# Loading x in two halves, turning its first tiles one by one, keeping router logits in PSUM, and a new order on four engines

## What is computed

```python
mod = silu(c) @ wmod                      # six vectors of 128: sa, ca, ga, sb, cb, gb
ga = (2 * (ga >= 0) - 1) * max(abs(ga), 0.25)   # and the same for gb
h = layernorm(x) * (1 + ca) + sa
q = (h @ Wq + bq) / sqrt(128); k = h @ Wk + bk; v = h @ Wv + bv
x = x + ga * (softmax(causal(q @ k.T)) @ v @ Wo + bo)
h = layernorm(x) * (1 + cb) + sb
mask = top 4 of 16 blocks of softmax(h @ w_router + b_router)   # per token
y = relu(h @ w1.T + b1) * mask_per_channel @ w2.T + b2          # 16 blocks of 32 channels
x = x + gb * y
```

## Time and profile before

| What | Value |
|---|---|
| Time, median of 3 runs (lowest to highest) | 119.22 us (119.22 to 119.25) |
| The profiled execution's own time | 119.25 us |
| Its span in the profile | 117.4 us |
| Busy PE, PEld | 111.6 us (95%), 87.7 us (75%) |
| Busy DVE, ACT, POOL | 89.6 us (76%), 76.0 us (65%), 88.8 us (76%) |
| Chain that ended last, by engine | PE 60%, DVE 21%, POOL 6%, issue 4%, ACT 3%, DMA 3% |
| DMA | 3.42 MB, nearly all of the reading in the first 10.5 us |

### The profile page before, as it was taken

The page is one execution under the profiler, slowest core; times in us unless marked ns, Lnnn a source line. Parts: engine busy times, 40 slices in busy tenths (PEclk is TensorE's granted clock), DMA queues, the critical chain, the costliest instruction groups (busy, mean ns, idle before and its releaser), DMA issues.

```text
span 117.4 us, 1999 instructions
## 1 busy us (share of the span) xinstructions
PE 111.6 (95%) x587; PEld 87.7 (75%) x587; DVE 89.6 (76%) x312; ACT 76.0 (65%) x162; POOL 88.8 (76%) x122
## 2 busy tenths in 40 slices
PE   5999998999999999999999999999998999999980
PEld 2488777877888888878787878778777887855770
DVE  5579999998898989999895489715898836894431
ACT  2326887768945697975889997498632696436430
POOL 6587979679996999999969999959992897812000
PEclk9999999999999999999999999999999999999999
DMA  1994000000000000000000000000000000006033
GB/s 39 244 366 115 3 0 0 6 3 0 3 0 0 6 0 0 0 0 3 0 0 0 6 0 0 0 0 0 0 0 6 3 0 3 0 0 179 6 89 89
DMA packets 6274, 3.42 MB, mean 29 GB/s; under 512 B 1141, under 2 KB 5878, under 8 KB 6263
## 3 DMA queue, kind: packets, MB, share of 16 engines
q1 hardware_dynamic: 5830, 3.09, 9.1%
q10 hardware_dynamic: 432, 0.20, 0.6%
HBM read 2.24 MB, written 1.05 MB: 28 GB/s over the span
## 4 chain that ended last, share of the span: by engine, by line
PE 60%; DVE 21%; POOL 6%; issue 4%; ACT 3%; DMA 3%; DVEq 0%; ACTq 0%
PE bank L841 16%; PE bank L845 14%; PE bank L842 14%; PE bank L884 6%; PE bank L955 3%; DMA cols<-in_L_c_dram 3%; DVE chosen L755 2%; POOL p_lo L467 2%; DVE swung_sums L729 2%; DVE marked L747 2%; DVE hid_full L764 2%; DVE keys L738 1%; DVE st L629 1%; PE bank L1043 1%; PE bank L865 1%
## 5 line engine op out<-in xcount | busy, mean ns | idle before, releaser
L467 POOL TENSOR_TENSOR p_lo<-p_full,p_hi 128x512 fp32r<-128x512 f32 (+2 forms) x36 | 43.3, 1224 | 5.1 <-ACT p_full L570 5.1
L563 ACT ACTIVATE p_hi<-bank 128x512 fp32r<-128x512 f32 (+2 forms) x36 | 20.6, 572 | 6.9 <-PE bank L845 3.0
L570 ACT ACTIVATE p_full<-bank 128x512 f32<-128x512 f32 (+2 forms) x36 | 20.6, 572 | 2.5 <-POOL p_lo L467 2.4
L473 POOL TENSOR_TENSOR hid_lo<-hid_full,hid_hi 128x512 fp32r<-128x512 f32 x12 | 15.4, 1290 | 6.1 <-ACT hid_hi L597 6.0
L669 DVE TENSOR_REDUCE cmax<-bank 128x1 f32<-128x512 f32 x24 | 16.2, 685 | 1.1 <-PE bank L884 0.6
L841 PE MATMUL bank<-g_hi,zt_hi 128*128 128x512 f32 (+3 forms) x40 | 15.1, 379 | 0.4 <-DVE back L802 0.4
L884 PE MATMUL bank<-zt_hi,g_hi 128*128 128x512 f32 (+3 forms) x40 | 15.0, 391 | 0.1
L845 PE MATMUL bank<-g_lo,zt_hi 128*128 128x512 f32 (+3 forms) x40 | 14.6, 365 | 0.0
L842 PE MATMUL bank<-g_hi,zt_lo 128*128 128x512 f32 (+3 forms) x40 | 14.6, 364 | 0.0
L841 PE MATMUL bank<-p_hi,z_hi 128*128 128x512 f32 (+2 forms) x36 | 14.1, 392 | 0.0
L845 PE MATMUL bank<-p_lo,z_hi 128*128 128x512 f32 (+2 forms) x36 | 13.5, 376 | 0.0
(11 more groups left out here) (190 smaller groups left out, 259.0 us busy)
## 6 DMA issues: line engine op xcount, KB each, us to landing
x<-in_L_attn_y_all_dram SPq DMA_DIRECT2D x4, 256.0 KB, 3.8
out_dram<-res SPq DMA_DIRECT2D x3, 256.0 KB, 2.4
w<-in_L_ffn_w_dram SPq DMA_DIRECT2D x2, 256.0 KB, 4.7
wmod<-in_L_wmod_dram SPq DMA_DIRECT2D x1, 256.0 KB, 4.5
out_dram<-res SPq DMA_DIRECT2D x2, 128.0 KB, 1.8
wmod<-in_L_wmod_dram ACTq DMA_DIRECT2D x1, 128.0 KB, 3.7
wk<-in_L_attn_Wk_dram SPq DMA_DIRECT2D x1, 64.0 KB, 3.3
wq<-in_L_attn_Wq_dram ACTq DMA_DIRECT2D x1, 64.0 KB, 3.5
```

The costliest lines, as they stand in the source:

```text
L467: pool.tensor_tensor(p_lo[:, s, w:], p_full[:, n % 2, w:], p_hi[:, s, w:].bitcast(F32), ALU.subtract).then_inc(p_lo_pool, 1)
L473: pool.tensor_tensor(hid_lo[:, m, :], hid_full[:, n % 2, :], hid_hi[:, m, :].bitcast(F32), ALU.subtract).then_inc(hid_lo_pool, 1)
L563: nc.scalar.activation(p_hi[:, s, w:], src, ACT.Exp).then_inc(p_hi_s, 1)
L570: nc.scalar.activation(p_full[:, n % 2, w:], src, ACT.Exp).then_inc(p_full_s, 1)
```

## The change

x of group 0 is loaded by two DMAs of two tiles each, the first with a semaphore of its own. The statistics of tiles 0 and 1 wait for the first, those of tiles 2 and 3 for the second. VectorE's a0 raises a semaphore after each tile, and TensorE's n0 waits tile by tile. The router's logits are written into a free part of the PSUM bank that holds the sums, in place of the SBUF tensor `logit`, and read from there. All four plans are replaced; TensorE's has four filler words fewer (i12 to i15).

```diff
@@ -39,30 +39,28 @@
 UNDER = -87.33
 
 TENSOR_PLAN = """
-i0 i1 i2 z0 i3 i4 i5 i6 i7 z1 i8 i9 i10 i11 i12 i13 i14 i15 z2 z3 n0 z6 z8 z4 q0 n1 a0 a1 z9 a2 q1 a3 z7 a4 b0
-z5 a5 n2 a6 a7 s0 a8 a9 s1 q2 a10 s2 a11 w0 a12 s3 b1 w1 a13 n3 a14 s4 a15 w2 a16 s5 a17 a18 s6 a19 s7 a20 w3
-a21 s8 a22 s9 a23 w4 s10 w5 o0 w6 q3 s11 b2 w7 a24 w8 a25 s12 a26 w9 a27 s13 a28 s14 a29 w10 a30 w11 s15 s16
-a31 s17 a32 w12 a33 w13 s18 o1 s19 n4 w14 a34 a35 s20 w15 w16 a36 s21 a37 s22 a38 w17 a39 w18 s23 w19 b3 w20
-r0 w21 s24 w22 w23 s25 s26 h0 s27 m0 w24 s28 n5 s29 o2 s30 w25 s31 w26 r1 s32 w27 h1 w28 s33 s34 w29 m1 w30
-w31 s35 s36 n6 s37 h2 w32 h3 s38 s39 r2 w33 w34 w35 w36 w37 w38 w39 h4 h5 m2 d0 o3 d1 d2 d3 h6 h7 d4 d5 y0 h8
-h9 d6 n7 h10 h11 r3 d7 h12 d8 d9 m3 y1 h13 v12 v13 d10 d11 h14 v14 h15 v15 d12 d13 d14 y2 d15 d16 d17 d18 d19
-y3 y4
+i0 i1 i2 z0 i3 i4 i5 i6 i7 z1 n0 i8 i9 z2 i10 i11 z6 z3 z8 q0 z9 n1 a0 z4 a1 a2 q1 a3 z5 a4 z7 a5 b0 a6 n2 a7
+s0 a8 a9 s1 q2 a10 s2 a11 w0 a12 s3 b1 w1 a13 n3 a14 s4 a15 w2 a16 s5 a17 s6 a18 w3 a19 s7 s8 o0 w4 s9 w5 a20
+a21 s10 q3 a22 w6 a23 w7 a24 w8 b2 s11 a25 w9 w10 a26 s12 a27 s13 a28 w11 a29 s14 a30 s15 a31 s16 w12 o1 w13
+s17 s18 a32 a33 w14 s19 a34 a35 s20 w15 s21 a36 w16 a37 n4 a38 s22 s23 a39 w17 w18 w19 b3 w20 r0 w21 s24 w22
+s25 w23 s26 s27 w24 m0 o2 s28 n5 s29 w25 w26 h0 s30 s31 r1 s32 h1 s33 w27 w28 w29 s34 m1 h2 s35 w30 n6 w31 s36
+h3 h4 s37 r2 s38 w32 s39 w33 w34 w35 w36 h5 w37 w38 w39 d0 d1 o3 d2 m2 d3 h6 h7 d4 d5 y0 h8 h9 d6 n7 d7 h10 r3
+d8 d9 y1 h11 m3 h12 h13 v12 v13 d10 d11 h14 v14 h15 v15 d12 y2 d13 d14 d15 d16 d17 d18 d19 y3 y4
 """
 SCALAR_PLAN = """
-z0 z1 z3 n0 a1 q0 n1 z4 z6 z12 q1 a2 z9 z5 z8 n2 e0 q2 e1 a3 e2 e3 e4 n3 e5 e6 c0 e7 e8 q3 e9 e10 e11 e12 e13
-e14 c1 e15 a4 e16 e17 z7 e18 e19 e20 e21 n4 e22 a5 e23 e24 c2 e25 e26 m0 e27 e28 n5 e29 e30 h0 e31 e32 a6 h1
-e33 m1 e34 e35 n6 e36 e37 e38 h2 h3 e39 c3 h4 h5 y0 m2 h6 h7 a7 h8 n7 h9 h10 y1 h11 m3 h12 h13 y2 h14 h15 y3
-y4
+z0 z1 n0 z3 z6 a1 q0 n1 z8 z4 q1 z5 a2 z9 z12 n2 e0 e1 q2 a3 e2 e3 e4 n3 e5 c0 e6 e7 e8 e9 q3 e10 e11 e12 e13
+c1 e14 e15 e16 e17 e18 a4 e19 e20 e21 z7 n4 e22 e23 a5 e24 c2 e25 e26 m0 e27 e28 n5 e29 e30 h0 e31 a6 e32 e33
+h1 m1 e34 e35 n6 h2 e36 e37 e38 e39 h3 c3 h4 h5 m2 y0 h6 h7 a7 h8 n7 h9 y1 h10 m3 h11 h12 h13 y2 h14 h15 y3 y4
 """
 VECTOR_PLAN = """
-g0 z1 g1 a0 g2 z10 z3 z11 n0 g3 q0 s0 n1 s1 s2 s3 q1 s4 b0 s5 z5 s6 s7 n2 s8 s9 s10 s11 s12 b1 s13 s14 s15 s16
-s17 s18 s19 s20 s21 s22 i8 s23 n3 q2 x0 i9 i10 b2 s24 i11 s25 s26 s27 s28 g4 s29 s30 s31 q3 s32 s33 z6 x1 g5
-s34 s35 i20 s36 s37 i21 s38 s39 i22 n4 b3 i23 m0 c0 h0 x2 n5 g6 m1 c1 h1 i36 n6 h2 i37 i38 h3 m2 i39 c2 h4 h5
-x3 g7 h6 h7 h8 h9 n7 h10 m3 c3 h11 f0 f1 k12 k13 k14 k15 f2 f3 f4
+g0 z1 a0 g1 n0 g2 z3 z10 z11 g3 q0 s0 n1 s1 s2 s3 q1 s4 z5 s5 b0 s6 s7 n2 s8 s9 s10 s11 s12 b1 s13 s14 s15 s16
+s17 s18 s19 q2 n3 i8 x0 i9 s20 s21 i10 s22 s23 s24 b2 s25 i11 s26 s27 s28 s29 s30 s31 g4 q3 x1 z6 s32 s33 g5
+s34 i20 s35 s36 i21 s37 s38 i22 i23 s39 n4 b3 m0 c0 x2 n5 g6 h0 m1 c1 h1 h2 n6 i36 h3 m2 i37 h4 i38 i39 c2 h5
+x3 g7 h6 h7 h8 h9 n7 h10 m3 c3 f0 h11 f1 k12 k13 k14 k15 f2 f3 f4
 """
 GPSIMD_PLAN = """
-z7 z0 z1 z5 z4 p0 p1 p2 u0 z6 p3 u1 l0 l1 z8 l2 u2 l4 l5 u3 l6 l7 z11 l8 l9 l10 z10 l12 l13 p4 l14 l15 l16 l17
-l18 p5 l19 l20 l21 l22 z9 l24 l25 l26 l27 l28 l29 l30 p6 k0 l31 l32 l33 l34 l35 k1 l36 l37 l38 k2 k3 k4 k5 p7
+z0 z5 p0 z1 z7 p1 u0 z6 p2 z8 u1 p3 l0 l1 z4 l2 u2 l4 l5 l6 l7 l8 l9 l10 z11 u3 z10 l12 l13 l14 l15 l16 p4 l17
+l18 l19 p5 l20 l21 l22 z9 l24 l25 l26 l27 l28 l29 p6 l30 l31 k0 l32 l33 k1 l34 k2 l35 l36 l37 l38 k3 k4 k5 p7
 k6 k7 k8 k9 k10 k11
 """
 
@@ -214,7 +212,6 @@
 
 
         swung_sums = sb("swung_sums", [P, GT, 2, NBLK])
-        logit = sb("logit", [P, GT, NBLK])
         lmax = sb("lmax", [P, GT])
         keys = sb("keys", [P, GT, KEYS])
         top8 = sb("top8", [P, GT, 8])
@@ -226,6 +223,7 @@
             sem(n) for n in ("c_loaded", "wmod1_loaded", "wmod2_loaded", "wq_loaded", "wk_loaded", "wv_loaded", "wo_loaded"))
         bias_qk_in_s, bias_vo_in_s, w1_in_s, b1_in_s, w2_in_s, wr_in_s, b2_in_s = (
             sem(n) for n in ("bias_qk_loaded", "bias_vo_loaded", "w1_loaded", "b1_loaded", "w2_loaded", "router_loaded", "b2_loaded"))
+        x_first_s, first_applied = sem("x_first_loaded"), sem("first_applied")
         stored = [sem(f"stored{g}") for g in range(NG)]
 
         ident_made, copies_made, causal_made, future_made, unseen_made, warm_made, filler_made, base_made, ones_made, keys_made, spread_made = (
@@ -280,8 +278,10 @@
             return grp(first if n < NG else second, n % NG)
 
         def norm_applied(n):
+            if n == 0:
+                return first_applied, GT
             by_act = scalar_applies(n)
-            return xn_by_act if by_act else xn_by_dve, sum(scalar_applies(k) == by_act for k in range(n + 1))
+            return xn_by_act if by_act else xn_by_dve, sum(scalar_applies(k) == by_act for k in range(1, n + 1))
 
         def one_turn(g):
             return g in ONE_TURNS
@@ -343,7 +343,8 @@
             def load_x(g):
                 load(tokens(x, g), x_tiles[g], x_in_s[g])
 
-            load_x(0)
+            for i in range(2):
+                load(x[:, 2 * i:2 * i + 2, :], x_tiles[0][:, 2 * i:2 * i + 2, :], x_in_s[0] if i else x_first_s)
             load(wk[:], wk_in, wk_in_s)
             load_column(BQ, bq_in, bias_qk_in_s)
             load_column(BK, bk_in, bias_qk_in_s)
@@ -621,11 +622,13 @@
             def norm_stats(n):
                 k, g = n // NG, n % NG
                 s = slice(g * GT, (g + 1) * GT)
-                if k == 0:
+                if n > 0 and k == 0:
                     dve.wait_ge(x_in_s[g], 16)
-                else:
+                elif k == 1:
                     dve.wait_ge(turn_out, turn_of[f"o{g}"] + 2)
                 for i in range(GT):
+                    if n == 0 and i % 2 == 0:
+                        dve.wait_ge(x_in_s[0] if i else x_first_s, 16)
                     last = nc.vector.bn_stats(st[:, k, g * GT + i, :], x[:, g * GT + i, :])
                 step(last)
                 for i in range(GT):
@@ -645,7 +648,10 @@
                     t = g * GT + i
                     last = nc.vector.tensor_scalar(norm_rows(n)[:, i, 1:], x[:, t, 1:], mv[:, k, t, 0:1],
                                                    rstd[:, k, t:t + 1], ALU.subtract, ALU.mult)
-                last.then_inc(xn_by_dve, 1)
+                    if n == 0:
+                        last.then_inc(first_applied, 1)
+                if n > 0:
+                    last.then_inc(xn_by_dve, 1)
 
             def norm_low(n):
                 dve.wait_ge(nt_hi_s, n + 1)
@@ -732,10 +738,11 @@
                     sums = swung_sums[:]
                 if g == 0:
                     dve.wait_ge(keys_made, 1)
-                step(nc.vector.tensor_reduce(logit[:], sums.rearrange("p i s e -> p i e s"), AX.X, ALU.add))
-                step(nc.vector.tensor_reduce(lmax[:], logit[:], AX.X, ALU.max))
+                logit = sums_bank(g)[:, GW // 2:GW // 2 + GT * NBLK].rearrange("p (i e) -> p i e", i=GT)
+                step(nc.vector.tensor_reduce(logit, sums.rearrange("p i s e -> p i e s"), AX.X, ALU.add))
+                step(nc.vector.tensor_reduce(lmax[:], logit, AX.X, ALU.max))
                 most = lmax[:].rearrange("p (i o) -> p i o", o=1).broadcast_to([P, GT, NBLK])
-                nc.vector.scalar_tensor_tensor(out=keys[:, :, 0:NBLK], in0=most, scalar=UNDER, in1=logit[:], op0=ALU.add,
+                nc.vector.scalar_tensor_tensor(out=keys[:, :, 0:NBLK], in0=most, scalar=UNDER, in1=logit, op0=ALU.add,
                                                op1=ALU.max).then_inc(keys_s, 1)
 
             def choose(g):
@@ -850,18 +857,21 @@
                     pe.wait_ge(turn_out, n - 1)
 
             def turn_norm(n):
-                pe.wait_ge(*norm_applied(n))
-                if n == 0:
+                if n > 0:
+                    pe.wait_ge(*norm_applied(n))
+                else:
                     pe.wait_ge(ident_made, 1)
                     pe.wait_ge(ones_made, 1)
-                elif n < NG:
+                if 0 < n < NG:
                     pe.wait_ge(nt_lo_s, n)
                 elif n == NG:
                     pe.wait_ge(nt_lo_s, NG)
                     pe.wait_ge(ones_made, 2)
-                else:
+                elif n > NG:
                     pe.wait_ge(keep_s, n - NG)
                 for i in range(GT):
+                    if n == 0:
+                        pe.wait_ge(first_applied, i + 1)
                     last = nc.tensor.transpose(tile(norm_bank, i), norm_rows(n)[:, i, :], ident[:])
                 last.then_inc(xt_mm, 1)
 
```

## The result

The changed kernel takes 118.78 us, median of 12 runs (118.48 to 120.4), against 119.27 us for the kernel before in the same session. The ratio is 0.9952, with a 95% interval of 0.9934 to 0.9970. The forecast was 119.7 us and slower; the kernel became 0.5% faster. The profiled execution took 118.82 us with a span of 117.1 us.

The account below looks back on a forecast made before the run. A GpSimd, VectorE and ScalarE chain bounds up to TensorE's first score s0, then TensorE's fixed work plus waits. 119.25 + 1.45 - 1.09 + 0.15 = 119.76 us, 0.03 above the median, so 119.7 us predicted; range 118.4 to 120.7.

Parts of the forecast that it names:

- the named late waits: TensorE's waits for group 2's choice, group 3's choice and ScalarE's copy of the latter: 0.47, 0.40, 0.22 us, all to go.
- The start: Up to TensorE's first score s0: g1 behind a0 delays p1, a1 and q0; s0 +1.45 us, at 20.4, bounds +0.75 to +1.9.
- the block of lift1 by GpSimd: VectorE's z1 at the start: lift1 waits for p0's power operation until 6.98, so a0 starts at 7.45; 0.45 us.
- the rest of the reordering behind s0: Order changes after the first score that rows couldn't cost: taken as 0, between -0.5 and +0.5 us.
- The waits from q0 to s0: Steps in the way on ScalarE and TensorE may make q1 late ahead of s0: 0.25 us, between 0 and 0.7.
- The late weight: SyncE's later loads: one weight TensorE now wants earlier (w1, for z6) may come late, priced at 0.3 us.
- The gain meant for the path: At the start, a0 ahead of g1 lets n0's high half start after about 8.9 in place of 10.17, over 1 us.
- After s0: Behind the first score: named waits go, -1.09 us, at the least -0.2; new waits +0.15; other reordering 0.
- The new wait of 0.15 us at h13: On TensorE, h13 needs h11's bank, and f0 (0.7 us) stands ahead of h11 on VectorE: +0.15 us.
- (1): Rival: GpSimd bounds the middle since z4 falls into it and late low halves hold TensorE; 120.7 us, chance 0.16.
- (2): Rival: faster, new order removes TensorE's many small waits between 20 and 113 us, exceeding s0's loss; 118.4 us, chance 0.27.
- (3): Rival: lift1 isn't blocked, a0 starts at 7.0, s0 +1.0 us; end 119.15 us, no difference that can be told, chance 0.15.

Follow-up runs that it names:

- the square: Four kernels, logits in PSUM, start and rest each old or new: old/old 118.87 us, old/new 118.11, new/old 119.48, new/new (the changed kernel) 118.78.
- the run with g1 first: Changed kernel with one swap on VectorE, the statistics g1 again ahead of a0: 119.32 us, ratio 0.9996 to the kernel before.
- the whole load: Changed kernel with x of group 0 loaded by one DMA again, all else as changed: 119.01 us, ratio 0.9979 to the kernel before.
- the run with a0 first: Kernel with PSUM logits and new orders only behind router step r0, plus p0 ahead of z4 and a0 ahead of g1: 118.56 us, ratio 0.9936.
- all old orders: Changed kernel with all four orders of the kernel before; half loads, tile by tile transposes and PSUM logits remain: 118.99 us, ratio 0.9967.
- p0 first: Kernel with PSUM logits and new orders only behind router step r0, plus p0 ahead of z4 on GpSimd: 117.99 us, ratio 0.9889.
- the crossed runs: Two kernels with PSUM logits, plans exchanged at TensorE's s0: kernel before with new plans behind it, 118.11 us; changed kernel with old plans behind it, 119.48 us.
- old start and new rest: Kernel before with PSUM logits and the changed kernel's plans from TensorE's first score s0 on: 118.11 us, ratio 0.9898 to the kernel before.
- new from r0 on: Kernel before with PSUM logits and new orders only behind TensorE's router step r0: 117.70 us, ratio 0.9867 to the kernel before.
- the second splice: Kernel before with PSUM logits, new order from s0 to score s15, old order from there to r0, new behind: 122.30 us, ratio 1.0224.
- new start and old rest: Changed kernel up to TensorE's first score s0, then the plans of the kernel before, with PSUM logits: 119.48 us, ratio 1.0013.

## Why the prediction was wrong

**What bounds the kernel** was right: what s0 loses the end loses, as the square shows, and the named late waits were on the path.

**Which steps failed.** Two terms of the sum were wrong, both towards a slower kernel. The start was put at +1.45 us and measured +1.01 in the trace and 0.6 to 0.7 in the medians; within it the block of lift1 by GpSimd, 0.45 us, didn't take place. And the rest of the reordering behind s0 was put at nothing, where the trace shows some 0.4 us of gain, group 1's choice and the turn of norm 6 above all. In the traces either error alone would have left about no change (+1.45 - 1.36 = +0.09, +1.01 - 0.94 = +0.07), and both together give the gain. In the medians the start alone turns the sign (+0.6 - 0.94 = -0.3).

**The start** had the right sign and, but for the block, the right mechanism, and was mis-sized. Forecast for s0 was +1.45 us (bounds 0.75 to 1.9); the trace shows +1.01, and medians of whole runs 0.6 to 0.7. Step by step: a0 was put at 7.45 and came at 7.15, g1's end at 9.80 and came at 9.45, a1 at 12.0 and came at 11.53. The step that failed is the block of lift1 by GpSimd's power operation, 0.45 us. In the run with g1 first lift1 started at 5.90, took 0.36 us and ended well inside the power operation of 5.61 to 6.66: no block. With the whole load it is the same (lift1 from 6.47 for 0.36 us, the power operation from 6.25 to 7.30), and so with lift2 in the run with a0 first (from 10.85 for 0.34 us, inside the operation of 10.25 to 11.29). In the changed kernel itself the two don't overlap: lift1 started at 6.81, after the power operation's end at 6.68, and was late for another reason, TensorE's first preparation. The row on which I priced it, the keys operation, is a wait for an operation on 128x512; the power operation is on 128x4. The rule of the Trainium skill (SBUF — State Buffer, section Who interferes with whom), that a VectorE instruction with two SBUF inputs contends with a GpSimd instruction that reads SBUF, fits keys, which was held with two such inputs and took 0.22 us each time with one of them in PSUM. For lift1, which names one SBUF tensor twice, these traces don't agree with it. Whether the double name or the small operation is the reason wasn't tried. The two may not be wholly free of each other: where lift1 began 0.12 or 0.13 us ahead of the power operation, the latter took 1.14 and 1.13 us in place of 1.05 (all old orders, p0 first). The waits from q0 to s0, taken at 0.25 us, measured 1.01 - 0.79 = 0.22. Why whole runs lose less than the first score isn't shown; the last section has what the rows say.

That x of group 1 is covered held for the changed kernel, whose g1 doesn't wait for it. The late weight priced at 0.3 us came: in the changed kernel TensorE waits 0.37 us for w1 at 9.74, and in the old orders 0.30 us for wmod. That either moves s0 isn't shown, and the first hardly can, for q0 comes only at 11.51. The gain meant for the path, a0 1.1 us earlier, was worth nothing, as said.

**After s0** the forecast was -1.09 of named waits and +0.15 of new ones, -0.94 us together. Measured from s0 to y4: -1.36 by the trace (-0.35 - 1.01), and -1.1 by the medians (logits 0.4 and rest 0.7). The three named waits went, but they were worth 0.9 and not 1.09, since for two of them 0.23 us was taken as the distance without a wait where it is 0.32. The new wait of 0.15 us at h13 didn't come (104.43 stands 0.24 us behind 104.19). Left out was group 1's choice, and the turn of norm 6 behind it. In the kernel before:

```profile
73.61 1.46 DVE L755 TENSOR_SCALAR chosen<-marked 128x512 bf16<-128x512 f32 x1
...
74.66 0.39 PE L845 MATMUL bank<-p_lo,z_hi 128*128 128x512 f32 x1
75.13 0.40 PE L991 MATMUL bank<-ident_b,chosen 128*128 128x128 bf16 x4
...
78.19 0.60 PE L865 MATMUL bank<-ident,xn 128*128 128x128 f32 x4
78.83 0.45 PE L841 MATMUL bank<-g_hi,zt_hi 128*128 128x384 f32 x1
```

Here chosen takes 1.46 us, where it takes 0.43 in the changed kernel, and m1 waits 0.47 - 0.23 = 0.24 us for it. Behind the turn of norm 6 the next product comes after 0.64 us, in the changed kernel after 0.35. From r0 to m1 the changed kernel saves 0.44 us, and from m1 to n7 0.8 where 0.47 was counted. Both waits could have been costed from the kernel before as the three were; that the first would go could not, since it hangs on the 0.09 us by which chosen comes ahead of GpSimd. The other way there was a loss, 0.44 us from s0 to r0.

**The rivals.** (1) z4 in GpSimd's full stretch costs nothing against z8: the crossed runs stay in step. The loss from s0 to r0 was there, though, 0.44 us; part of it is one wait for a low half, the mechanism of this rival with another cause. TensorE's third pass comes at 59.07, 0.52 us behind the second (58.55), so 0.29 us late; p5, which the new order has one low half later, ends at 57.78 on GpSimd, just ahead of that half. In the list of waits of the changed kernel between 48 and 62 us it stands with the weight load (us in total, times, longest):

```profile
PEld bank L852 <- POOL p_lo L468: 0.6, 1, 0.6
```

The rest of that loss stays open. (2) was right in kind: the waits saved after s0 exceeded what s0 lost. It was given 118.4 us and a chance of 0.27. (3) was right that lift1 isn't blocked and that s0 moves by 1.0 us, and its time of 119.15 was nearer than the forecast; what it lacked is the gain of the reordering behind r0. With the distances of the trace in place of the terms the sum is 119.25 + 1.01 + 0.44 - 0.44 - 0.81 - 0.55 = 118.90. That it comes within 0.1 us of the profiled 118.82 is no test of the account, since the five distances add up to the shift of y4.

## What to carry to other kernels

When whole orders change, compare the start times of steps ahead of which both orders have done the same set of work; each stretch between them can be priced and swapped by itself, and the best of both may beat either. A splice has to keep every chain that runs over several engines in one order. Moving a step out of a hole to bring another forward pays only if nothing behind it waits for the step that was moved. Cost every wait of the bounding engine of the same kind (here all the choices and the turns of the norms), not only the largest ones, and take the distance without a wait from a product of the same form.

## What the hardware showed beyond that

The early clock of TensorE moves the start. Its filler products of 512 columns start 0.43 us apart at first (2.07, 2.50, 2.92 in the changed kernel), twice the 0.23 us of later products; 512 columns in 0.427 us are 1.2 in a ns, so this is the 1.2 GHz level, although the granted clock is written as 1.00 there. In the run with g1 first seven of them take 2.70 us in place of 3.19 in the changed kernel's profile (TensorE's timeline, this run and then the changed kernel):

```profile
2.50 2.70 PE L1116 MATMUL bank<-filler 128*128 128x512 bf16 x7
```

```profile
2.50 3.19 PE L1116 MATMUL bank<-filler 128*128 128x512 bf16 x7
```

TensorE's first preparation stands behind them, and lift1 comes at 5.90 in place of 6.81. So the spacing narrows earlier in one run than in the other, with the same orders on TensorE. Runs of equal starts differ too: with the old start lift1 came at 6.48, 6.04 and 6.84 us and s0 at 18.98, 18.80 and 19.23 (before, old start and new rest, new from r0 on). The clock isn't all of it, for in the second splice, with the same start, lift1 came at 6.20 and s0 at 19.50. This is of the size of the differences looked for here, and one profile of a start can be off by it. The profiled executions were also not the medians of their runs: 117.71 us against 118.11 for old start and new rest, 119.66 against 119.48 for new start and old rest. That accounts for the 1.0 to 1.2 us of the start in the profiles beside the 0.6 to 0.7 in the medians by size, but no run fixed the moment of the rise, so its part in it isn't shown. Fewer fillers, or a preparation ahead of them, may take it off the path; that wasn't tried.
